# The last batch's FFN split by token tile, orders remade on every engine, and fewer warm-up matmuls in a decoder kernel

## The reference: one decoder layer

```
x = x + linear_attention(layernorm(x))                 # 16 heads of 8, phi = elu + 1
x = x + softmax_attention(layernorm(x), ctx)           # causal, 16 heads of 8
h = layernorm(x)
scores = sigmoid(h @ Wr); top 2 of 8 experts, weights normalised -> cw
hid = silu(h @ Wg[e]) * (h @ Wu[e])                    # e = 0..3, 64 wide each
x = x + sum_e cw[e] * hid[e] @ Wd[e]
      + (cw[4] + cw[6]) * h + cw[7] * relu(h)
      + depthwise_causal_conv(h, 4 taps)
```

## Time and profile before

| | |
|---|---|
| median of 3 runs | 182.6 us (182.4 to 182.61) |
| the profiled execution's own time | 182.75 us |
| its span, first to last instruction | 181.0 us |
| PE, DVE, ACT, POOL busy | 169.6, 160.6, 127.8, 118.3 us |
| last instruction on DVE (`finish.7.0`) begins | 178.28 us |
| last store issued on SP | 178.73 us |

### The profile page before, as it was taken

How to read it: one execution, slowest core, us unless ns; L and a number is a source line. 1 busy time by engine, 2 the same in 40 slices (tenths; PEclk the granted TensorE clock), 3 DMA queues, 4 the chain that set the end, 5 groups by cost and what they waited for, 6 DMA issues and landing times. The chain is left out here.

```text
span 181.0 us, 5282 instructions
## 1 busy us (share of the span) xinstructions
PE 169.6 (94%) x1898; PEld 119.3 (66%) x1898; DVE 160.6 (89%) x448; ACT 127.8 (71%) x289; POOL 118.3 (65%) x248
## 2 busy tenths in 40 slices
...
GB/s 175 222 320 41 5 61 81 89 50 45 78 61 91 40 55 63 46 59 81 85 57 63 33 51 71 38 107 87 2 4 0 5 31 4 2 29 4 29 2 58
DMA packets 17929, 10.97 MB, mean 61 GB/s; under 512 B 2656, under 2 KB 17248, under 8 KB 17904
## 3 DMA queue, kind: packets, MB, share of 16 engines
...
...
## 5 line engine op out<-in xcount | busy, mean ns | idle before, releaser
L752 DVE TENSOR_REDUCE negmax<-max_pair 128x4 f32<-128x1024 f32 (+1 forms) x48 | 58.4, 1217 | 4.3 <-PE max_pair L862 3.8
L622 ACT ACTIVATE probs<-soft_pair 128x1024 f32<-128x1024 f32 x48 | 49.3, 1026 | 12.9 <-PE soft_pair L862 12.7
L521 POOL TENSOR_SCALAR_AFFINE_SELECT probs<-probs 128x512 f32<-128x512 f32 (+1 forms) x48 | 37.6, 796 | 15.6 <-ACT probs L622 15.6
L862 PE MATMUL pv_bank<-probs,vs 128*32 128x256 f32 (+1 forms) x448 | 21.1, 329 | 0.1
L862 PE MATMUL soft_pair<-qs,ks 64*128 64x256 bf16 (+1 forms) x256 | 18.8, 245 | 0.4 <-DMA qs<-maxparts 0.3
L536 POOL TENSOR_TENSOR hid<-hraw,cw 128x256 f32<-128x256 f32 x16 | 10.5, 661 | 12.9 <-DVE cw L806 10.7
L495 POOL TENSOR_TENSOR rstd<-vareps,exponent 128x2 f32<-128x2 f32 x24 | 17.5, 728 | 2.0
L862 PE MATMUL max_pair<-ks,qs 64*128 64x128 bf16 (+1 forms) x256 | 18.4, 242 | 0.0
L862 PEld LDWEIGHTS pv_bank<-probs,vs 128*32 128x32 f32 x448 | 12.8, 109 | 7.2 <-issue 1.7
L862 PE MATMUL max_pair<-causal,picks 64*128 64x128 bf16 (+1 forms) x192 | 15.2, 237 | 1.6 <-DVE negmax L752 0.8
L565 ACT ACTIVATE xn<-inputs,shift,rstd 128x128 f32<-128x128 f32 x32 | 14.1, 492 | 3.1 <-POOL shift L497 3.1
...
## 6 DMA issues: line engine op xcount, KB each, us to landing
...
out_dram<-result SPq DMA_DIRECT2D x8, 128.0 KB, 1.8
...
qs<-maxparts SPq DMA_DIRECT2D x32, 4.0 KB
...
```

Of the source, the lines that this page charges most:

```text
L521: nc.gpsimd.affine_select(out=v, in_=v, compare_op=ALU.is_ge, fill=0.0, base=0, pattern=[[0, n], [1, P]], channel_multiplier=-1).then_inc( ...
L622: nc.scalar.activation(probs[b.par][g][:, k, :], soft_pair[:, :], ACT.Exp).then_inc(exp_done, 1)
L752: nc.vector.tensor_reduce(maxima, max_pair[:, :].rearrange("p (u h k) -> p u h k", u=2, h=n), AX.X, ALU.max, negate=True).then_inc(max_rea ...
L862: return nc.tensor.matmul(out, lhsT, rhs, start=start, stop=stop, skip_group_check=True)
```

## The change

For the last batch (`LAST = 7`) four steps are made once for each token tile: `ffn_hid_t` (two transposes), `hidT` (a copy of 256 columns), `ffn_down`, `finish` (128 columns) and `store_out` (64 KB). The second tile uses the bank that `ffn_gate_up.7.1` had (`up.7`). The waits behind them count one step more.

All five lists of `ORDER` are written anew. The steps are the same but for the five added ones and the warm-ups, and most differ by a few places. In the last stages seven warm-ups remain, in four places, of 26 in nine; three single ones are added near the start. Three waits are added: `zero_max` waits for the scores of the batch that had the buffer before, `norm3` for `relu7` two batches back, `act_q` for `phi_q` two batches back.

```diff
+LAST = B - 1
 "sp":
-  load.0.0 load.0.1 load.0.2 load.0.6 load.0.3 load.0.4 load.0.5 hi_k.0.0 mid_k.0.0 lo_k.0.0 hi_q.0.0 mid_q.0.0
-  lo_q.0.0 load.0.7 hi_k.1.0 ...
-  ... send_max.0.0 hi_q.2.0 hi_k.2.0 mid_k.2.0 send_max.0.1 mid_q.2.0 lo_k.2.0 send_max.1.0 lo_q.2.0 hi_q.3.0 ...
-  ... store_out.5.0 store_out.6.0 store_out.7.0
+  load.0.0 load.0.1 load.0.2 load.0.6 load.0.3 hi_k.0.0 load.0.4 load.0.5 mid_k.0.0 lo_k.0.0 hi_q.0.0 mid_q.0.0
+  lo_q.0.0 hi_k.1.0 ...
+  ... send_max.0.0 hi_k.2.0 hi_q.2.0 load.0.7 send_max.0.1 mid_q.2.0 mid_k.2.0 lo_k.2.0 lo_q.2.0 hi_q.3.0 send_max.1.0 ...
+  ... store_out.5.0 store_out.6.0 store_out.7.0 store_out.7.1
 "pool":
-  ... sig.4.0 mask.7.0 mask.7.1 hid.4.0 hid.4.1 mask.7.2 mask.7.3 conv.5.0 sig.5.0
-  mask.7.4 mask.7.5 base.4.0 rstd3.6.0 conv.6.0 hid.5.0 hid.5.1 rstd3.7.0 sig.6.0 base.5.0 hid.6.0 hid.6.1 sig.7.0
-  conv.7.0 hid.7.0 hid.7.1 base.6.0 base.7.0
+  ... sig.4.0 mask.7.0 hid.4.0 hid.4.1 mask.7.1 mask.7.2 conv.5.0 sig.5.0 mask.7.3
+  mask.7.4 mask.7.5 base.4.0 rstd3.6.0 hid.5.0 conv.6.0 hid.5.1 sig.6.0 rstd3.7.0 base.5.0 conv.7.0 hid.6.0
+  sig.7.0 hid.6.1 hid.7.0 hid.7.1 base.6.0 base.7.0
 "act":
-  ... tanh_g.7.0 tanh_g.7.1 hidT.6.0 hidT.7.0 relu7.7.0
+  ... tanh_g.7.0 tanh_g.7.1 hidT.6.0 relu7.7.0 hidT.7.0 hidT.7.1
 "dve":
-  ... finish.4.0 skip.5.0 skip.5.1 div2.7.0 div2.7.1
-  gate.5.1 times_up.5.1 tap.5.2 route.6.0 route.6.1 x2.7.0 route.6.2 stats3.7.0 var3.7.0 gate.6.0 tap.6.0 tap.6.1
-  route.6.3 times_up.6.0 route.6.4 tap.6.2 route.6.5 gate.6.1 route.6.6 route.6.7 skip.6.0 finish.5.0 times_up.6.1
-  route.7.0 route.7.1 route.7.2 route.7.3 route.7.4 route.7.5 gate.7.0 route.7.6 times_up.7.0 route.7.7 gate.7.1
-  times_up.7.1 tap.7.0 skip.6.1 skip.7.0 tap.7.1 tap.7.2 finish.6.0 skip.7.1 finish.7.0
+  ... finish.4.0 route.5.6 route.5.7 tap.5.2 div2.7.0 div2.7.1 skip.5.0
+  skip.5.1 gate.5.1 times_up.5.1 x2.7.0 route.6.0 stats3.7.0 var3.7.0 tap.6.0 route.6.1 tap.6.1 route.6.2 gate.6.0
+  route.6.3 tap.6.2 route.6.4 times_up.6.0 route.6.5 route.6.6 gate.6.1 finish.5.0 route.6.7 times_up.6.1 skip.6.0
+  tap.7.0 route.7.0 route.7.1 route.7.2 route.7.3 route.7.4 route.7.5 gate.7.0 route.7.6 times_up.7.0 route.7.7
+  gate.7.1 times_up.7.1 skip.6.1 tap.7.1 skip.7.0 tap.7.2 skip.7.1 finish.6.0 finish.7.0 finish.7.1
 "pe":
-  ... ffn_gate_up.4.1 soft.7.2
-  ffn_x_t.5.0 out_t.6.0 warm.7.2 soft.7.3 ffn_router.5.0 warm.7.2 ffn_hid_t.4.0 o2_t.6.0 soft.7.4 pv.7.0 soft.7.5
-  o_proj.6.0 ffn_gate_up.5.0 ffn_down.4.0 pv.7.1 ffn_gate_up.5.1 out_t.7.0 warm.7.1 ffn_x_t.6.0 o2_t.7.0
-  ffn_router.6.0 o_proj.7.0 ffn_gate_up.6.0 ffn_hid_t.5.0 ffn_gate_up.6.1 ffn_down.5.0 warm.7.3 ffn_x_t.7.0
-  warm.7.1 ffn_router.7.0 warm.7.1 ffn_gate_up.7.0 ffn_gate_up.7.1 ffn_hid_t.6.0 warm.7.3 ffn_down.6.0 warm.7.1
-  ffn_hid_t.7.0 warm.7.5 ffn_down.7.0
+  self_x_t.0.0 self_q1.0.0 warm.0.1 cross_k.0.0 warm.0.1 self_kv.0.0 ... self_sum.1.0 warm.0.1 self_x_t.4.0 ...
+  ... ffn_gate_up.4.1 ffn_x_t.5.0 soft.7.2 warm.7.1 out_t.6.0 soft.7.3 ffn_hid_t.4.0 ffn_router.5.0
+  o2_t.6.0 soft.7.4 ffn_down.4.0 soft.7.5 o_proj.6.0 ffn_gate_up.5.0 pv.7.0 pv.7.1 ffn_gate_up.5.1 out_t.7.0
+  ffn_x_t.6.0 warm.7.2 o2_t.7.0 ffn_router.6.0 o_proj.7.0 ffn_gate_up.6.0 ffn_hid_t.5.0 ffn_gate_up.6.1
+  ffn_down.5.0 ffn_x_t.7.0 warm.7.2 ffn_router.7.0 ffn_gate_up.7.0 ffn_gate_up.7.1 ffn_hid_t.6.0 ffn_down.6.0
+  warm.7.2 ffn_hid_t.7.0 ffn_hid_t.7.1 ffn_down.7.0 ffn_down.7.1
...
+        def half_bank(b, t):
+            return bank_of[f"up.{b.c}"] if t else bank("ffn", b)
...
             def zero_max(b, _):
                 if b.since(4):
+                    sp.wait_ge(pe_soft, b.count(UNITS, -3 * UNITS))
...
-                sp.dma_start(out_v[b.c], result[b.par][:, :, :]).then_inc(out_stored[b.par], 16)
+                if b.c == LAST:
+                    sp.dma_start(out_v[b.c, :, t], result[b.par][:, t, :]).then_inc(out_stored[b.par], 16)
+                else:
+                    sp.dma_start(out_v[b.c], result[b.par][:, :, :]).then_inc(out_stored[b.par], 16)
...
+                act.wait_ge(pe_hid_t, b.count(1, t + 1))
+                if b.c == LAST:
+                    nc.scalar.copy(hidT[b.par][:, :, t * P:(t + 1) * P],
+                                   half_bank(b, t)[:, 0:2 * P].rearrange("p (i s) -> p i s", i=2)).then_inc(hidT_done, 1)
+                    return
...
+            def finish(b, t):
+                dve.wait_ge(pe_down, b.count(1, t + 1))
                 dve.wait_ge(base_done, b.count(1, 1))
...
+                if b.c == LAST:
+                    nc.vector.tensor_tensor(result[b.par][:, t, :], half_bank(b, t)[:, 0:C], base[b.par][:, t, :], ALU.add).then_inc(result_done, 1)
+                    return
...
+            def ffn_down(b, half):
+                pe.wait_ge(hidT_done, b.count(1, half + 1))
                 pe.wait_ge(taps_done, b.count(KC - 1, KC - 1))
+                for t in [half] if b.c == LAST else range(T):
+                    o = half_bank(b, t)[:, 0:C] if b.c == LAST else bank("ffn", b)[:, t * C:(t + 1) * C]
```

More of the change, by code:

```diff
@@ new lines @@
+        mask.1.0 bias.7.0 mask.1.1 rstd2.5.0 mask.1.2 rstd2.6.0 rstd3.0.0 mask.1.3 mask.1.4 mask.1.5 mask.2.0 sig.0.0
+        lo_k.4.0 mask.2.1 lo_q.4.0 rstd2.7.0 conv.0.0 mask.2.2 lo_k.5.0 hid.0.0 mask.2.3 mask.2.4 hid.0.1 mask.2.5
+        rstd3.1.0 base.0.0 lo_q.5.0 mask.3.0 mask.3.1 conv.1.0 mask.3.2 mask.3.3 mask.3.4 sig.1.0 mask.3.5 hid.1.0
+        hid.1.1 lo_k.6.0 rstd3.2.0 lo_q.6.0 base.1.0 mask.4.0 mask.4.1 mask.4.2 mask.4.3 conv.2.0 mask.4.4 mask.4.5
+        sig.2.0 hid.2.0 lo_k.7.0 hid.2.1 lo_q.7.0 rstd3.3.0 base.2.0 mask.5.0 mask.5.1 mask.5.2 conv.3.0 mask.5.3
@@ L56 @@
+        mask.5.4 mask.5.5 mask.6.0 sig.3.0 mask.6.1 mask.6.2 hid.3.0 hid.3.1 rstd3.4.0 base.3.0 mask.6.3 mask.6.4
+        conv.4.0 mask.6.5 rstd3.5.0 sig.4.0 mask.7.0 hid.4.0 hid.4.1 mask.7.1 mask.7.2 conv.5.0 sig.5.0 mask.7.3
+        mask.7.4 mask.7.5 base.4.0 rstd3.6.0 hid.5.0 conv.6.0 hid.5.1 sig.6.0 rstd3.7.0 base.5.0 conv.7.0 hid.6.0
+        sig.7.0 hid.6.1 hid.7.0 hid.7.1 base.6.0 base.7.0
     """,
     "act": """
-        norm1.0.0 xnT.0.0 act_q.0.0 hi_k.0.0 norm1.1.0 act_kv.0.0 xnT.1.0 norm1.2.0 act_q.1.0 mid_k.0.0 xnT.2.0
@@ L74 @@
[L74 to L77 removed]
+        norm1.0.0 xnT.0.0 act_q.0.0 hi_k.0.0 norm1.1.0 act_kv.0.0 xnT.1.0 mid_k.0.0 norm1.2.0 act_q.1.0 xnT.2.0
@@ new lines @@
+        div2.1.0 route.0.4 div2.1.1 route.0.5 reduce.3.3 gate.0.0 max_mid.3.0 x2.1.0 times_up.0.0 reduce.3.4 route.0.6
+        tap.0.0 route.0.7 gate.0.1 reduce.3.5 times_up.0.1 rest_q.5.0 stats3.1.0 reduce.4.0 max_mid.3.1 skip.0.0
+        var3.1.0 tap.0.1 reduce.4.1 tap.0.2 skip.0.1 reduce.4.2 finish.0.0 rest_k.6.0 reduce.4.3 max_mid.4.0 div2.2.0
+        tap.1.0 div2.2.1 route.1.0 reduce.4.4 route.1.1 tap.1.1 gate.1.0 reduce.4.5 route.1.2 times_up.1.0 route.1.3
+        x2.2.0 route.1.4 reduce.5.0 max_mid.4.1 route.1.5 rest_q.6.0 route.1.6 gate.1.1 route.1.7 times_up.1.1
@@ new lines @@
+        cross_q2.5.0 ffn_gate_up.0.1 soft.2.4 max.3.5 pv.2.0 soft.2.5 max.4.0 cross_k.6.0 maxrow.3.1 ffn_hid_t.0.0
+        max.4.1 soft.3.0 pv.2.1 soft.3.1 max.4.2 ffn_down.0.0 soft.3.2 max.4.3 ffn_x_t.1.0 cross_v.6.0 maxrow.4.0
+        out_t.2.0 ffn_router.1.0 max.4.4 soft.3.3 ffn_gate_up.1.0 o2_t.2.0 cross_norm_t.6.0 soft.3.4 max.4.5 o_proj.2.0
+        cross_q2.6.0 soft.3.5 max.5.0 ffn_gate_up.1.1 maxrow.4.1 pv.3.0 soft.4.0 max.5.1 pv.3.1 soft.4.1 max.5.2
+        cross_k.7.0 ffn_hid_t.1.0 out_t.3.0 soft.4.2 max.5.3 ffn_down.1.0 maxrow.5.0 max.5.4 ffn_x_t.2.0 cross_v.7.0
```

189 lines of the change are left out of this document (93 added, 96 removed).

## The result

The changed kernel takes 181.64 us (median of 18 runs, 181.41 to 182.28), the kernel before 182.58 us (18 runs, 182.38 to 183.07). The ratio is 0.9951 (95%: 0.9943 to 0.9958), so 0.9 us (0.8 to 1.0) were gained where 0.6 were forecast: the sign was right, the time lies inside the range, and the gain is over half as large again. The granted clock was 0.998 to 1.0 in all 18. The profiled execution took 181.51 us, its span is 179.77 us.

The account below looks back on a forecast made before the run. PE was taken to set the end up to about 160 us, DVE from 164.07. The last store 0.46 us earlier and 0.1 for a smaller last transfer take 0.56 off the median 182.6: 182.0, range 181.5 to 182.4.

Parts of the forecast that it names:

- Part 5: Order of all steps not priced elsewhere: taken as 0, bounded at 0.9 us on either side.
- Part 1: Fewer PE warm-ups: those in the softmax stretch give 0.55 us, `x2.7` at about 163.5; the others nothing.
- Part 2: DVE from `x2.7` to `route.7.0`: 6.7 us (6.33 to 7.24) against 6.07 before; `route.7.0` starts at 170.2.
- Part 3: DVE from `route.7.0` to the end of `skip.7.1`: 7.18 us before, now ending at 176.56.
- Part 4: Splitting the last batch's final steps: earns about 0.1 us; the last store leaves at 178.27, 0.46 us earlier.
- The clock falls: PE's clock falls to half rate in the last stages: 2.5 us lost, 184.5; chance 0.10.
- The tail gain is eaten: DVE reaches `route.7.0` 0.5 us later, so the end is within 0.1 of before, 182.5; chance 0.20.
- SP's queue: Near the start, `send_max.1.0` behind four DMAs makes `soft.1.0` wait: up to 1 us lost, 183.0; chance 0.12.
- More is gained: `x2.7` to `route.7.0` at its lower sum (-0.4) and earlier gaps close by 0.5: 181.1; chance 0.13.
- the middle: DVE's stretch between 30 and 146 us: reordering there taken as 0; `x2.5` moving over 0.9 us would refute it.

Follow-up runs that it names:

- all_warm: The changed kernel with all 19 warm-ups of the tail back in nine places, as in the kernel before; ratio 0.9968 to the kernel before.
- new_head: The kernel before with the changed kernel's lists up to about 145 us, then the old order, old warm-ups and no split; ratio 0.9968 to the kernel before.
- x2_early: The changed kernel with the chain to `x2.7` put first (`o2_t.7` ahead of `ffn_x_t.6` and its warm-ups, steps on ACT and DVE moved); ratio 0.9927 to the kernel before.
- no_split: The changed kernel with batch 7's FFN whole again, order and warm-ups as changed; ratio 0.9966 to the kernel before.
- skip_early: The changed kernel with `skip.6.1` moved ahead of `tap.7.0` on DVE; its end is 0.23 us earlier than the changed kernel's.
- old_head: The changed kernel with every engine's list up to about 145 us in the order of the kernel before; ratio 0.9978 to the kernel before.

## Why the prediction was right, and where it was short

The sign and the range were right, and the total was near for reasons that are partly luck: one term was missing (part 5), one had the wrong sign (part 1), and parts 2 to 4 were larger than forecast.

**Part 5, the order of everything else, is the term that was mis-sized most.** It was taken as 0 within 0.9 us either way; measured it is 0.58 us (0.35 to 0.84), the larger part of the gain. "The swaps are small and as many open a gap as close one" is the sentence that failed. The row to look for was there, in a stretch from which none was read; DVE's timeline of the kernel before has it:

```profile
135.42 1.07 DVE L840 SCALAR_TENSOR_TENSOR conv<-x3T,inputs,conv 128x256 f32<-128x256 f32 x1
```

It is `tap.3.1`, over twice as long as a tap alone (0.47), in front of the last steps of `route.3`.

**Part 1.** Warm-ups in the softmax stretch were priced at 0.55 us for `x2.7`. They bring 0.23 (all_warm), and the new order around them takes more than that away: order and warm-ups together make `x2.7` 0.24 later (new_head). What the forecast left out is on PE. Before, `o2_t.7` stood behind one warm-up and `ffn_x_t.6`, which started without a wait. Now `ffn_x_t.6` waits 0.93 us for `norm3.6`, and two warm-ups stand between it and `o2_t.7`; x2_early, which puts `o2_t.7` first (and moves some steps of ACT and DVE with it), gets 0.69 back. `x2.7` came at 163.43 as forecast (163.5) by luck: from 164.07, 0.28 is the delay in the profile of before, 0.60 the head's gain (from 163.79 to the 163.19 of new_head), and 0.24 was lost again. The count of warm-ups was wrong too, 26 and 19 fewer where there are 19 and 12 fewer; that made PE's saving 4.2 us instead of 2.6, which no term of the sum uses. The three in front of `ffn_x_t.7` and the five in front of `ffn_down.7` were said to be "Worth nothing there"; with everything around them earlier they cost 0.17 and 0.16 (all_warm). They were priced at the old state of their neighbours.

**Part 2.** From `x2.7` to `route.7.0`: 6.55 us, forecast 6.7 in 6.33 to 7.24. The 0.49 idle went, the tap ran beside `hid.6.0` for 0.82 us, as expected. Not expected: DVE idles 0.74 us in front of it. The steps ahead of it make up for that: `route.6.4` takes 0.19 us where it took 0.61, and `route.6.0` and `route.6.1` came cheap at 0.26 (163.77 to 163.88, 164.94 to 165.09). `route.7.0` at 169.98, forecast 170.2.

**Part 3.** From `route.7.0` to the end of `skip.7.1`: 6.02 us, forecast 6.36. 0.1 was allowed for alternating taps and skips, 0.4 was found. The route steps up to `times_up.7.1` give 0.16 of it (3.22 us against 3.38). The two taps take 0.78 us from start to next start where they took 1.41, which gives 0.63, and `skip.6.1` with the gap behind it gives 0.18. `base.6` (from 174.23, before 174.94) now falls beside `skip.7.0`, a small step, which it stretches to 0.68 us; that takes 0.53 back.

**Part 4.** The split was given 0.1 us and earns about 0.3 (no_split). The argument was that `ffn_down.7.0` waits for the taps, not for `hidT`. It does, in the changed kernel: the half copy is there at 175.24, the last tap at 175.48, and `ffn_down.7.0` starts at 175.62 (the copy that the record names had been done). But the whole copy would be there only at 175.69 (175.86 in no_split, less 0.17 of start), so without the split `hidT` would be last. Again the taps were taken at their old time. The step from store to end of span is 2.04 us (179.77 - 177.73) instead of 2.27, 0.13 more than the 0.1 allowed.

So in the tail the sizes were off in both directions: part 1 was too large by 0.8 (0.55 forecast, 0.24 lost), parts 2 to 4 too small (from `x2.7` to the end of the last `finish` 14.55 us forecast, 14.63 before, 14.10 measured). The errors cancel, and so the forecast sum of 0.56 us lies inside what the tail alone measured, 0.40 (0.18 to 0.62). The total is short by what the head gave.

**The rivals.** *The clock falls* did not happen in the changed kernel in 18 runs, but it is real: six of twelve executions without the seven warm-ups. The forecast price of 2.5 us was somewhat above the worst case, 1.5 to 2.2. *The tail gain is eaten* was not the case (tail alone 0.9978), though its mechanism is what keeps x2_early and skip_early from adding. *SP's queue*: no sign; `reduce.2.0` starts no later than before. *More is gained* is the way it went, by the middle and not by part 2: 181.64 lies between the forecast's 182.0 and that rival's 181.1, and still in the forecast's own range of 181.5 to 182.4.

**What would show it.** The last store was forecast between 178.1 and 178.4 and is at 177.73, a sign that failed; `route.7.0` at 169.98 is inside its 169.9 to 170.6; "no idle DVE before `route.6.4`" and "`x2.7` near 163.5" hold; "`base.7` ends last before `finish.7.0`" holds (176.88 against 176.53). `x2.5` moved by 0.92, just over the 0.9 that was named as the sign that the middle had been misjudged. It was the right place to look, but the limit was too wide: 0.28 of it is the delay in the profile of before, and against old_head (143.94) `x2.5` moved by 0.64.
